# Routing of the second layer's experts: a stage of its own, or a part of the attention's batch loop

## The reference, cut to what matters

```python
x = x + _L1_xattn_ref(_layernorm(x, axis=-1), ctx_2048, ...)   # 16 x 128 tokens
x = x + _L1_ffn_ref(_layernorm(x, axis=-1), L1_ffn_router_w, L1_ffn_w1, L1_ffn_w2)
...
logits = xf @ router_w.T                       # 2048 x 8
topk_vals, topk_idx = jax.lax.top_k(logits, K) # K = 2 of 8 experts
topk_w = jax.nn.softmax(topk_vals, axis=-1)
order = jnp.argsort(exp_id)
x_sorted = xf[order // K]                      # rows grouped by expert
y1 = jax.lax.ragged_dot(x_sorted, jnp.swapaxes(w1, 1, 2), counts)
y_act = jax.nn.silu(gate) * up
y2 = jax.lax.ragged_dot(y_act, jnp.swapaxes(w2, 1, 2), counts)
```

## Time and profile before

| what | us |
|---|---|
| median of 3 runs (3263.78 to 3267.24) | 3264.55 |
| the profiled execution, its own time | 3265.82 |
| its span in the profile | 3263.6 |
| busy, PE / DVE / ACT / POOL | 2882.3 / 1810.2 / 1693.0 / 1744.4 |

### The profile page before, as it was taken

How to read it: one execution, slowest core, us unless ns; L and a number is a source line. 1 busy time by engine, 2 the same in 40 slices (tenths; PEclk the granted TensorE clock), 3 DMA queues, 4 the chain that set the end, 5 groups by cost and what they waited for, 6 DMA issues and landing times. The chain is left out here.

```text
span 3263.6 us, 57383 instructions
## 1 busy us (share of the span) xinstructions
PE 2882.3 (88%) x16324; PEld 1652.9 (51%) x16325; DVE 1810.2 (55%) x5172; ACT 1693.0 (52%) x4502; POOL 1744.4 (53%) x2429
## 2 busy tenths in 40 slices
PE   4699999999999699999999996799989999625996
PEld 2366666666666445555555542344444444423663
DVE  4366666666666464334444353688888888321331
ACT  5577778778777433332333242566666666311331
POOL 6467777777776344434554453655655565240222
PEclk8799999999999899999999998999999999657998
DMA  6601101111110255544554474455555555327444
GB/s 236 232 27 43 43 29 36 43 38 35 39 42 23 95 167 161 153 130 137 161 152 129 144 212 100 78 109 109 106 103 106 107 106 101 96 100 264 84 84 106
DMA packets 459854, 348.33 MB, mean 107 GB/s; under 512 B 295728, under 2 KB 366512, under 8 KB 459696
## 3 DMA queue, kind: packets, MB, share of 16 engines
q1 hardware_dynamic: 396896, 267.79, 29.4%
q0 software_dynamic: 16640, 38.05, 5.8%
q10 hardware_dynamic: 46224, 41.36, 4.3%
HBM read 194.88 MB, written 93.50 MB: 88 GB/s over the span
## 5 line engine op out<-in xcount | busy, mean ns | idle before, releaser
L751 ACT ACTIVATE a_nrm<-a_mm,a_sc_t 128x128 f32<-128x128 f32 x768 | 291.4, 476 | 123.5 <-POOL a_sc_t L904 123.4
L1647 POOL TENSOR_TENSOR e_st<-e_st,e_ws_tile 128x1024 f32<-128x1024 f32 x64 | 123.5, 1930 | 427.4 <-PE e_y L1403 416.8
L602 DVE BATCH_NORM_STATS2 a_st<-a_mm 128x6 f32<-128x128 f32 x768 | 170.7, 284 | 291.2 <-PE a_mm L439 208.7
L438 PE MATMUL a_mm<-a_w_hi,a_xq_hi 128*128 128x512 f16 x768 | 297.4, 387 | 23.2 <-POOL a_xq_lo L886 15.0
L439 PE MATMUL a_mm<-a_w_hi,a_xq_lo 128*128 128x512 f16 x768 | 297.2, 387 | 0.0
L1441 ACT ACTIVATE e_hh<-e_ha 128x512 f16<-128x512 f32 x128 | 76.3, 596 | 414.7 <-PE e_ha L1388 413.5
L1536 DVE SCALAR_TENSOR_TENSOR e_hl<-e_ha,e_hh 128x512 f16<-128x512 f32 x128 | 88.5, 691 | 352.2 <-ACT e_hh L1441 351.8
L1812 PE MATMUL a_mm<-l_wh,a_src_hi 128*128 128x512 f16 x512 | 200.4, 392 | 76.0 <-DVE a_vl L1894 41.8
L903 POOL TENSOR_TENSOR a_sc_t<-a_sc_t,a_mhalf 128x4 f32<-128x4 f32 x192 | 204.3, 1064 | 117.8 <-DVE a_sc_t L609 117.5
L1401 PE MATMUL e_y<-e_w2h,e_hh 128*128 128x512 f16 x640 | 242.6, 379 | 0.0
L1402 PE MATMUL e_y<-e_w2l,e_hh 128*128 128x512 f16 x640 | 242.6, 379 | 0.0
(11 more groups left out here) (350 smaller groups left out, 8220.7 us busy)
## 6 DMA issues: line engine op xcount, KB each, us to landing
e_st<-in_w SPq DMA_DIRECT2D x128, 512.0 KB, 4.2
disp<-a_empty SPq DMA_DIRECT2D x16, 781.5 KB, 4.1
e_st<-in_w1b SPq DMA_DIRECT2D x32, 352.0 KB, 3.1
e_xb<-disp ACTq DMA_DIRECT2D x41, 260.5 KB, 2.7
disp<-a_empty SPq DMA_DIRECT2D x4, 2605.0 KB, 21.1
e_xb<-disp SPq DMA_DIRECT2D x40, 260.5 KB, 4.3
a_cx<-in_ctxT SPq DMA_DIRECT2D x32, 256.0 KB, 3.2
a_stage<-in_wprojT SPq DMA_DIRECT2D x16, 512.0 KB, 4.9
```

The lines of the kernel that those rows point to most:

```text
L438: pe.matmul(out, xq_hi[:, n, c, :], w_hi[:, t, c, :], start=(c == 0), stop=False)
L751: ins = act.activation(nrm[:, n % 2, i * P:(i + 1) * P], src[:, i * P:(i + 1) * P], ACT.Identity, bias=sc_t[:, n % 2, 3, i:i + 1], scale=s ...
```

## The change

The stage `norm_route` is gone. Its work is spread over the batch loop of `layer1_attention` as steps like those of the first attention, with two buffers `xr` for the rows that are scattered. So that a row's place is known before all batches are counted, each expert gets a region of T = 2048 rows in `disp` (row expert * T + place), and a table `row_of_tile`, made at the end, tells the experts where a tile begins; ScalarE reads it before each tile's load. `disp` grows with it, so the first attention fills 8 * 128 rows a batch where it filled 3 * 128. The projections get a third PSUM bank; `c_high` and `c_low` move from the sixth slot to the second, to the front of their plans; four batches stand ahead of the loop where two did. An expert's weights are reported after the transfers of the next expert are issued, and no longer after all.

```diff
-FILL = 3
+FILL = E
+PAD = E * T
@@ layer1_attention
-        MMB = [s.ps(f"mm{n}", [P, DM]) for n in range(2)]
+        MMB = [s.ps(f"mm{n}", [P, DM]) for n in range(MM_BANKS)]
+        RB = s.ps("rb", [P, DM])
@@ TensorE
+            def r_transpose(b, k, q):
...
+                pe.wait_ge(sem["r_norm"], b + 1)
+                for c in range(KT):
+                    mm = pe.transpose(RB[:, c * P:(c + 1) * P], xr[:, q, c * P:(c + 1) * P], ident[:])
+                mm.then_inc(sem["r_tr"], 1)
+            def r_logits(b, k, q):
+                pe.wait_ge(sem["r_t"], b + 1)
+                for c in range(KT):
+                    mm = pe.matmul(RB[:, 0:E], xrT[:, c * P:(c + 1) * P], wg[:, c, :], start=(c == 0), stop=(c == KT - 1))
+            def r_prefix(b, k, q):
+                pe.wait_ge(sem["r_mask"], b + 1)
...
-                              ("att", 5, pv), ("att", 6, out_project)], NJ1, SCORE1, None, 2)
+                              ("att", 5, pv), ("att", 6, out_project), ("end", 11, r_transpose), ("end", 13, r_logits),
+                              ("end", 15, r_prefix)], NJ1, SCORE1, None, 2, HEAD1)
@@ VectorE
+            def r_slots(b, k, q):
+                dve.wait_ge(sem["r_px"], b + 1)
+                for n in range(2):
+                    ins = dve.scalar_tensor_tensor(out=rhit, in0=iota_e, scalar=rbest[:, n:n + 1], in1=RB[:, 0:E],
+                                                   op0=ALU.is_equal, op1=ALU.mult, accum_out=rslot[:, n:n + 1])
...
-                               ("end", 7, final), ("in", 3, x_stats)], NJ1, SCORE1, ch, 2)
+                               ("end", 7, final), ("end", 7, r_stats), ("in", 3, x_stats), ("end", 14, r_scores), ("end", 16, r_inverse),
+                               ("end", 16, r_slots)], NJ1, SCORE1, ch, 2, HEAD1)
@@ ScalarE
-            run_pipeline(act, [("att", 2, p_high),
+            run_pipeline(act, [("in", 2, c_high), ("att", 2, p_high),
...
-                               ("in", 6, c_high)], NJ1, SCORE1, None, 2)
+                               ("end", 10, r_norm), ("end", 12, r_keep), ("end", 15, r_exp), ("end", 17, r_gates)],
+                         NJ1, SCORE1, None, 2, HEAD1)
@@ GpSimd
+            def r_scatter(b, k, q):
+                pool.wait_ge(sem["r_px"], b + 1)
...
+                for n in range(2):
+                    pool.indirect_dma_start(
+                        out=disp, out_offset=bass.IndirectOffsetOnAxis(ap=sidx[:, q, n:n + 1], axis=0),
+                        in_=xr[:, q, :], in_offset=None).then_inc(r_sent[q], 16)
+            run_pipeline(pool, [("in", 2, c_low), ("job", 0, scales), ("in", 3, x_scale), ("in", 5, tables), ("end", 8, r_scale),
+                                ("end", 18, r_scatter)], NJ1, SCORE1, ch, 2, HEAD1)
@@ layer1_experts, SyncE
-            for e in range(E):
-                sp.wait_ge(w_in[e], 64)
-                sp.sem_inc(w_ok, 1)
+                if e >= 1:
+                    sp.wait_ge(w_in[e - 1], 64)
+                    sp.sem_inc(w_ok, 1)
+            sp.wait_ge(w_in[E - 1], 64)
+            sp.sem_inc(w_ok, 1)
@@ layer1_experts, ScalarE
-                act.dma_start(xb[:, q, :], disp[bass.ds(i * P, P), :]).then_inc(x_in[q], 16)
+                at = act.value_load(row_of_tile[0:1, bass.ds(i, 1)], min_val=0, max_val=PAD)
+                act.dma_start(xb[:, q, :], disp[bass.ds(at, P), :]).then_inc(x_in[q], 16)
```

More of the change, by code:

```diff
@@ L148, in slot @@
                 continue
-            for late in range(3):
+            for late in range(4):
                 u = t + late * jobs - off
@@ L942, in _ @@
             pool.wait_ge(scattered, 32 * B)
[L946 to L968, removed]
@@ L1209 @@
 SCORE1 = [6, 8, 10, 12]
+HEAD1 = 2
+BANK1 = [t % MM_BANKS for t in range(NJ1)]
+BEFORE1 = [max(u for u in range(-NJ1, t) if BANK1[u % NJ1] == BANK1[t]) for t in range(NJ1)]
 KEYS = 2 * P
@@ L1816, in project @@
             def project(b, t, q):
-                if not is0(b, t, 2):
-                    bb, tt = (b, t - 2) if t >= 2 else (b - 1, t - 2 + NJ1)
+                if not (is0(b, t, NJ1) and BEFORE1[t] < 0):
+                    bb, tt = (b, BEFORE1[t]) if BEFORE1[t] >= 0 else (b - 1, BEFORE1[t] + NJ1)
                     if tt in norm_no:
@@ new lines, in r_scores @@
+            def r_scores(b, k, q):
+                dve.wait_ge(sem["r_lgt"], b + 1)
+                dve.tensor_copy(rlg, RB[:, 0:E]).then_inc(sem["r_lg"], 1)
+                dve.wait_ge(sem["r_lg"], b + 1)
+                ch.add(dve.tensor_reduce(rnb, rlg, AX_X, ALU.max, negate=True))
+                ch.link(dve.max(rtop, rlg))
+                dve.max_index(rix[:], rtop, rlg).then_inc(sem["r_top"], 1)
+                dve.wait_ge(sem["r_top"], b + 1)
+                ch.link(dve.tensor_copy(rbest, rix[:, 0:2]))
+                ch.link(dve.tensor_scalar(roh, iota_e, rbest[:, 0:1], None, ALU.is_equal))
+                if not is0(b):
+                    dve.wait_ge(sem["r_sum"], b)
+                dve.scalar_tensor_tensor(out=rm[:, 0, :], in0=iota_e, scalar=rbest[:, 1:2], in1=roh,
+                                         op0=ALU.is_equal, op1=ALU.add).then_inc(sem["r_mask"], 1)
@@ new lines, in _ @@
+            tt, ts = dve.tensor_tensor, dve.tensor_scalar
+            start, count, whole, jump = (seg[:, n, :] for n in range(4))
+            ch.link(ts(count[:, 0:E], iota_e, -float(T), None, ALU.mult))
+            dve.wait_ge(sem["r_cnt"], 1)
+            ch.link(tt(count[:, 0:E], RB[:, E:2 * E], count[:, 0:E], ALU.add))
+            ch.link(ts(count[:, 0:E], count[:, 0:E], 1.0 / P, (P - 1.0) / P - 0.5 + 0.5 / P, ALU.mult, ALU.add))
+            ch.link(ts(whole[:, 0:E], count[:, 0:E], 1.5 * 2.0 ** 23, 1.5 * 2.0 ** 23, ALU.add, ALU.subtract))
@@ new lines, in _ @@
+            ch.link(dve.memset(start[:, 0:1], 0.0))
+            ch.link(ts(jump[:, 0:E], whole[:, 0:E], -float(P), float(T), ALU.mult, ALU.add))
+            for e in range(E):
+                ch.link(tt(start[:, e + 1:e + 2], start[:, e:e + 1], whole[:, e:e + 1], ALU.add))
+            ch.link(tt(te[:], tile_no.unsqueeze(2).to_broadcast([P, TILES, E]),
+                       start[:, 1:E + 1].unsqueeze(1).to_broadcast([P, TILES, E]), ALU.is_ge))
+            ch.link(dve.tensor_reduce(tef[:, 0, :], te[:, :, 0:E - 1], AX_X, ALU.add))
@@ L2323, in program @@
         expert_of_tile = s.sb("expert_of_tile", [1, TILES], I32)
+        row_of_tile = s.sb("row_of_tile", [1, TILES + 1], I32)
         tile_oh = s.sb("tile_oh", [P, TILES, E], F32)
```

311 lines of the change are left out of this document (114 added, 197 removed).

## The result

The changed kernel takes 3173.2 us (median of 4 runs, 3171.95 to 3175.2) beside 3265.25 us of the kernel before: a ratio of 0.9722, 95% interval 0.971 to 0.9734. That is faster by 92 us where 125 were forecast. It lies in the stated range, 33 us above the stated number, and between the forecast's own range (up to 3158) and rival B (3182).

What follows compares the result with a forecast made beforehand. The chain VectorE, ScalarE, GpSimd was taken to set the attention loop's period, with TensorE held up by it. −114.1 − 18.2 + 8 = −124.3 from the profiled 3265.8 gave 3141.5, forecast 3140 us; range 3098 to 3184.

Steps and rivals of the forecast that it cites:

- rival B: Attention loop: all of VectorE's routing is exposed, 3.6 us on each of 14 batches, 3182 us; chance 0.15.
- part 1: Stage between attention and experts: norm_route goes, 133.8 us become a tail of 19.7, saving 114.1 us.
- part 2: Experts' start: weights reported one expert on, up to 24.7 us earlier less 6 to 7 lost, net −18.2 us.
- the read of `row_of_tile`: ScalarE, before each tile's load in the experts: taken as nothing; beside the weights at most 4 us.
- part 3: Attention loop: routing steps, third bank and c_low's move together cost +0.6 us a batch, +8 us over 14.
- `r_stats`: VectorE in the attention loop, behind a_x3b with no wait behind it: +0.9 us a batch.
- The third bank: PSUM bank for the loop's projections: TensorE's waits for a_vl go, giving back only 0.15 us a batch.
- `c_low` leaving the place beside a_pql: Attention loop: a_pql runs faster without a_src_lo beside it; half of 1.87 us taken as gained, 0.9 a batch.
- rival D: Attention loop: a routing step ahead of its input stops an engine every batch, 14.2 us exposed, about 3330 us; chance 0.02.
- A: Attention loop: TensorE was the bound, the third bank frees 2.3 us a batch, about 3095 us; chance 0.12.
- C: Experts' start: rows wait behind weights, the 18.2 us gain falls to 1 to 9, 3149 to 3157 us; chance 0.05.
- E: Attention loop: scatters and VectorE hold each other up, 1.4 to 1.8 us a batch, 3162 us; chance 0.06.

Runs made afterwards that it cites:

- run 7: Kernel before with only the weights reported one expert on: 3248.5 us.
- run 5: Kernel before with the third PSUM bank and nothing else: 3260.0 us.
- run 2: Changed kernel with a batch's loads (rows and context) at the front of slot 0, split still in slot 2: 3153.0 us.
- run 4: Kernel before with c_high and c_low at the front of slot 2, third bank and loads at the front of slot 0, no routing in the loop: 3281.4 us.
- run 1: Changed kernel with c_high and c_low back at the end of slot 6: 3164.6 us.
- run 6: Changed kernel with loads at the front of slot 0, r_stats moved to slot 5 and r_scale following it: 3143.4 us.
- run 12: Changed kernel with loads in slot 0, r_stats in slot 5, weights one transfer at a time, c_high and c_low behind other steps of slot 2: 3129.0 us.
- run 3: Kernel before with c_high and c_low at the front of slot 2 and the third bank, no routing in the loop: 3301.9 us.

## Why the prediction was right, and where it was not

The direction, the stage and most of the weights came out by the mechanism that was given. The loop did not. The time lies outside the forecast's own range, and the stated range held it only because that left room for rival B, whose mechanism is not the one that was found: that part is luck.

**The stage** (part 1): 115.1 for 114.1. The tail of the first attention was a good model of the new one, and the tables ended 2.7 us ahead of the experts' first transfer, the very margin that was stated.

**The weights** (part 2): the mechanism, loads of rows behind weights, was right, and its size a little short: 8.9 us lost for 6 to 7, since six tiles met weights and not four. The 11.9 us to the first matmul for 9.8 come from a term that was put at nothing, the read of `row_of_tile`. In run 7, which has no such read, the first two loads of rows are issued 0.1 and 0.5 us behind the stage's first transfer:

```profile
2941.87 0.35 SPq L2165 DMA_DIRECT2D e_ident<-in_ident  x1
2941.96 0.85 ACTq L2229 DMA_DIRECT2D e_xb<-disp  x2
2942.27 0.43 SPq L2168 DMA_DIRECT2D e_w1h<-w1h  x1
```

In the changed kernel they are issued 1.0 and 2.1 us behind it (2862.63), the first after two weight transfers and the second after four:

```profile
2863.02 0.42 SPq L2105 DMA_DIRECT2D e_w1h<-w1h  x1
2863.49 0.43 SPq L2107 DMA_DIRECT2D e_w2h<-w2h  x1
2863.64 1.47 ACTq L2167 DMA_DIRECT2D e_xb<-disp  x2
2863.96 0.43 SPq L2105 DMA_DIRECT2D e_w1l<-w1l  x1
```

They take 6.8 and 7.5 us to land. Expert 0's weights are reported 9.9 us behind the stage's first transfer, but TensorE transposes tile 1 before it multiplies tile 0, and does so only at 10.5. By the traces the whole term is −24.8 + 7.0 = −17.8 in run 7, the forecast's −18.2, and −22.4 + 8.9 = −13.5 in the changed kernel. The 4.3 us between them are most likely the read with what it sets off, about the 4 us that the prediction named as the most it could add; no run takes the read out alone. Behind the weights it is hidden: the tiles are 6.3 us apart with it and without.

The loads of rows by source, in the stretch with weights (2863 to 2910) and behind it, answer to the earlier trace rows:

```profile
DMA to landing us min/median/max: 6.2/6.8/8.0
...
DMA to landing us min/median/max: 2.6/2.7/2.9
```

Alone the term measured 15.3 by the medians (run 7), inside its bounds.

**The loop** (part 3): the sum was +0.6 a batch and is +2.5. By its steps:
- `r_stats`, +0.9 and serial: measured 1.0, and taking it away gave back 1.1.
- `r_scores` nothing: the table of starts shows at most 0.1 for it. `r_inverse` and `r_slots` +0.4: nothing to be seen.
- The third bank −0.15: −0.15 by the distance of run 5, which is less than that measure can tell.
- `c_low` leaving the place beside a_pql, −0.9: here is **the step that failed**. The prediction costed what the split left, "In its new place it lies beside something else", and not what it came to wait for there. The load of the context is issued at the end of slot 1, right ahead, and at the front of ScalarE's order a_pqh, a_nrm and a_pr all stand behind the wait. This wait costs 1.3 a batch by run 2 and 1.5 by run 4. The question of when a step's input is there was asked of the routing's steps and not of this one.
- The gain that was put on it: a_src_lo was not alone beside that a_pql. Of the 1.87 us that the prediction gave to it, a part belongs to GpSimd's a_r, which runs beside the same four instructions and stays there. The first row is from the kernel before, the other three from the changed one:

```profile
2486.30 1.27 POOL L2104 TENSOR_TENSOR a_r<-a_r 128x512 f32<-128x512 f32 x1
2506.59 1.26 POOL L2018 TENSOR_TENSOR a_r<-a_r 128x512 f32<-128x512 f32 x1
2506.93 2.39 DVE L1772 SCALAR_TENSOR_TENSOR a_pql<-a_pr,a_ri,a_pqh 128x256 f16<-128x256 f32 x4
2508.87 1.11 POOL L2037 DMA_INDIRECT disp<-a_xr,a_sidx  x1 [0.29 <-POOL a_rsl L2035]
```

  So a_pql did lose 1.1 us of its 3.53 here, and 0.9 in other batches (3.3 to 2.4). The loop got little of it: in the table, the second a_nb, ahead of this a_pql, is 0.9 late and the second a_ol, behind it, still 0.7, and VectorE's wait for a_oh grew from 29.3 us in 32 to 52.2 in 41.
- Whether leaving pays depends on the rest. With the scatters in slot 6 the split may not stay there (run 1 against run 2: 49.3 and 48.1, so leaving is worth 1.2). Without them leaving costs 1.5 (run 4 against run 5: 48.2 and 46.7). In both pairs the place of the loads differs too.

So 1.1 (`r_stats`, run 6) and 1.3 (the wait, run 2) make up 2.4 of the 2.5, and with both taken away the loop is at 47.0, 0.1 above the kernel before.

Why leaving costs 1.5 without routing no run settles, but the trace of run 4 shows where it comes in. In GpSimd's slot 2 a_src_lo now stands ahead of a_sq, which starts straight behind it, without a wait:

```profile
2469.96 1.16 POOL L2073 TENSOR_TENSOR a_src_lo<-a_cx,a_src_hi 128x512 f16<-128x512 f32 x1
2471.08 0.20 POOL L2098 TENSOR_TENSOR a_sq<-a_st 128x8 f32<-128x8 f32 x1
2474.03 1.27 POOL L2106 TENSOR_TENSOR a_r<-a_r 128x512 f32<-128x512 f32 x1
2475.34 1.28 ACT L2010 ACTIVATE a_nrm<-a_r,a_sc 128x128 f32<-128x128 f32 x4 [3.08 <-POOL a_r L2106]
```

That a_r starts 42.2 us behind a_x3b, and 40.1 in run 5. ScalarE waits 3.1 us for it where it waited 1.3 in run 5, and a_pr, a_nqh and the a_oh of the last a_ol stand behind: in the table, run 4 is 0.2 late at the last a_nql and 1.5 at the last a_ol. It is the same kind of loss as in run 1, a moved step ahead of a late a_sq. What made GpSimd late already before that slot stays open.

One figure of the prediction does not follow from the sum beside it: rival D's "+199 less 124" gives 3340, and its 3330 is 3140 with 199 in place of 8. Nothing hangs on it.

**The rivals.** A is excluded by run 5. B had nearly the right number for the wrong reason: of VectorE's 3.6 us a batch only `r_stats` was exposed. C was true in a small part only: it left 1 to 9 us of the gain, and 13.5 are left by the trace and 15.3 in run 7. D's 14.2 us a batch did not come, but its mechanism did, a step that stands ahead of the main chain's work sooner than its input can be there; it came at `c_high`, which the prediction did not test for it, and at 1.3 us. E: the scatters took 956, 980 and 1127 ns (shortest, median, longest), none near 1477, and a_pql beside them 2.4 us and not 3.5:

```profile
L2037 POOL DMA_INDIRECT disp<-a_xr,a_sidx x32: 956/980/1127, 2212.1 to 2855.9; - x32
```

Nothing here shows the 3,100 ns that the Trainium skill (SBUF — State Buffer, "SBUF: two separate sides") gives for such a transfer beside a `tensor_copy` of VectorE. What E came near to, a_sq late behind the scatters, is what run 1 shows, and there only with the split in the same slot.

**Hidden at nothing**: the larger fill was (the last a_x1b at 1112.7 for 1113.5), and the clock stayed at 0.97.

## What to carry to other kernels

In a pipeline whose order is fixed by tables, cost a moved step by two questions: what it leaves, and what it waits for in the new place, with the issue of its load looked up in the other engine's order. A table of when each main instruction starts, counted from one fixed instruction of the loop, read side by side for two kernels, shows in which slot a batch loses its time; the sums of waits don't. When two edits act on the same slots, measure them together as well: here the same move went with +1.5 or −1.2 us a batch. And look at what a new read stands in front of: here a read of 0.9 us ahead of the first load of rows put it behind weight transfers, and it took 6.8 us to land where it had taken 2.9.

## What the runs showed of the hardware

VectorE and GpSimd hold each other up, for much of an instruction. In run 4, VectorE's a_nql starts just behind GpSimd's a_r and takes 1.73 us, as 10 of the 62 from 2200 to 2700 us do within 0.11 us, where the others take 0.67 to 0.72:

```profile
2460.69 1.26 POOL L2106 TENSOR_TENSOR a_r<-a_r 128x512 f32<-128x512 f32 x1
2460.77 1.73 DVE L1929 TENSOR_TENSOR a_nql<-a_nrm,a_nqh 128x512 f16<-128x512 f32 x1 [1.71 <-ACT a_nqh L2021]
```

GpSimd's ends at 2461.95, and 1.73 is the 1.18 us until then plus 0.55, a little less than the 0.69 of an undisturbed one. This is what the Trainium skill says (SBUF — State Buffer, "Who interferes with whom"): a VectorE instruction with both inputs in SBUF and a GpSimd instruction that reads SBUF lock each other out, for the whole of the one that came first. The trace agrees, with GpSimd's first by 0.08 us. GpSimd's side varies too: a_src_lo, always the same instruction, takes 1.16 us in run 4, 1.34 in the kernel before and 1.61 in run 12, each time in another place of the order. In the groups of VectorE from 2200 to 2700 us the same instruction is in run 4

```profile
L1929 DVE TENSOR_TENSOR a_nql<-a_nrm,a_nqh 128x512 f16<-128x512 f32 x62 | 52.6, 848 | 32.7 <-ACT a_nqh L2021 32.5
```

and in the changed kernel

```profile
L1753 DVE TENSOR_TENSOR a_nql<-a_nrm,a_nqh 128x512 f16<-128x512 f32 x61 | 42.0, 689 | 33.3 <-ACT a_nqh L1911 32.9
```

848 and 689 ns in the mean; in the changed kernel none of them takes over 0.73 us. The instruction is the same, and what differs is when it starts.

Take VectorE's three instructions with both inputs in SBUF (a_pql, a_nql, a_xql), and from each the shortest of its kind in any of the traces. What is left over is 4.7 us a batch in the kernel before and in run 4, 2.3 in the changed kernel and in run 2. It is tempting to say that the routing's instructions push the others out of step with GpSimd, and so hide some 2 us of their own price. That is not shown: run 1 has the routing and 4.1 us, run 3 has none and 3.6. The kernel with the lowest median (run 12) has 3.6 and a distance of 46.9, so the sum alone does not rank kernels either.
